# A one-column memset on GpSimd between any two of 6256 gathers in a four-round graph kernel

## What is computed

```python
h = relu(layernorm(x))
n1 = segment_sum(h[src], dst) / max(deg, 1)
n2 = segment_sum(n1[src], dst) / max(deg, 1)
x = x + 0.5 * n1 + 0.5 * n2
h = relu(layernorm(x))
for W_msg, W_edge, W_root, b in ((W1...), (W2...)):
    m = h[src] @ W_msg + edge_attr @ W_edge
    h = leaky_relu(where_finite(segment_max(m, dst)) + h @ W_root + b)
out = x + h
```

## Time and profile before

| | |
|---|---|
| median of 3 runs | 9557.13 us (9551.07 to 9563.12) |
| the profiled execution, its time | 9629.93 us |
| its span | 9628.2 us |
| granted TensorE clock, mean | 0.648 of full speed |
| busy share: TensorE matmul, VectorE, ScalarE, GpSimd | 58%, 34%, 16%, 67% |
| first to last gather of the four rounds | 61.0 to 2314.5, 2412.9 to 4651.5, 4777.2 to 7085.3, 7213.5 to 9521.9 us |

### The profile page before, as it was taken

One profiled execution on the slowest core, in us unless ns is written; L12 is line 12 of the kernel. 1 busy time (PEld: TensorE's weight loads), 2 busy tenths in 40 slices (PEclk: granted clock), 3 DMA queues, 4 the chain that ended last, 5 costly groups with the idle time before them and its releaser, 6 DMA issues.

```text
span 9628.2 us, 100471 instructions
## 1 busy us (share of the span) xinstructions
PE 5576.1 (58%) x25651; PEld 4095.6 (43%) x25651; DVE 3262.5 (34%) x6693; ACT 1500.7 (16%) x5073; POOL 6458.6 (67%) x6525
## 2 busy tenths in 40 slices
PE   2333333334233333333578877878887887887888
PEld 1222222223222222222555555555564555555556
DVE  4333333334333232323423333333332333333334
ACT  1000000001000000000322222222232222222223
POOL 5666666664666666666566666766656666666665
PEclk6555555556555555555767777777786777677776
DMA  3111111111111111111133333333323333333332
GB/s 79 35 34 34 34 34 34 34 35 39 47 35 34 34 34 35 34 34 35 46 76 77 77 77 77 78 80 78 77 64 71 80 78 77 77 77 77 77 81 64
DMA packets 309643, 548.56 MB, mean 57 GB/s; under 512 B 183464, under 2 KB 183464, under 8 KB 284712
## 3 DMA queue, kind: packets, MB, share of 16 engines
q0 software_dynamic: 200192, 307.90, 16.3%
q1 hardware_dynamic: 108804, 239.50, 9.7%
q10 hardware_dynamic: 548, 0.17, 0.0%
HBM read 522.27 MB, written 24.87 MB: 57 GB/s over the span
## 4 chain that ended last, share of the span: by engine, by line
another core or an unknown queue 29%; PE 26%; issue 9%; DVE 8%; DVEq 2%; ACT 1%; ACTq 1%; POOL 0%; DMA 0%; POOLq 0%; SPq 0%
PE ps L578 7%; PE ps L576 6%; PE ps L600 6%; PE ps L589 3%; DVE arena L799 3%; DVE comp L784 3%; PE ps L557 2%; DVE arena L767 2%; DVEq L257 1%; DVEq L784 1%; PE ps L662 1%; PE ps L638 0%; ACTq L257 0%; PE ps L675 0%
## 5 line engine op out<-in xcount | busy, mean ns | idle before, releaser
L374 POOL DMA_INDIRECT rows<-table,src_sb x6256 | 6273.4, 1003 | 2930.3 <-issue 1767.5
L557 PE MATMUL ps<-arena,rows 128*98 128x128 f32 (+1 forms) x6256 | 1418.1, 399 | 2967.0 <-DVE comp L784 2634.6
L557 PEld LDWEIGHTS ps<-arena,rows 128*98 128x98 f32 (+1 forms) x6256 | 1179.5, 254 | 3226.7 <-DVE comp L784 2836.3
L799 DVE TENSOR_TENSOR_SCAN arena<-arena,ps 96x512 f32<-96x512 f32 x782 | 996.6, 1274 | 3238.6 <-remote 1989.8
L784 DVE TENSOR_TENSOR comp<-comp,ps 98x128 f32 (+1 forms) x3128 | 893.6, 286 | 2878.4 <-remote 2317.0
L578 PEld LDWEIGHTS ps<-ident,rows 128*96 128x96 f32 x6256 | 950.4, 208 | 912.9 <-issue 912.7
L600 PE MATMUL ps<-arena 128*96 128x128 f32 x6256 | 1180.2, 352 | 108.6 <-issue 72.4
L578 PE MATMUL ps<-ident,rows 128*96 128x128 f32 x6256 | 1173.3, 344 | 54.2 <-issue 53.4
L576 PE MATMUL ps<-arena,we 32*96 32x512 f32 x1564 | 1143.7, 819 | 27.3 <-DMA rows<-table,src_sb 27.3
L600 PEld LDWEIGHTS ps<-arena 128*96 128x96 f32 x6256 | 1052.2, 228 | 129.6 <-issue 124.4
L767 DVE TENSOR_TENSOR arena<-iota_b,meta 128x512 f32<-128x512 bf16 x1564 | 1053.0, 673 | 59.6 <-issue 55.1
(11 more groups left out here) (84 smaller groups left out, 1026.0 us busy)
## 6 DMA issues: line engine op xcount, KB each, us to landing
arena<-flags SPq DMA_DIRECT2D x194, 768.0 KB
rows<-table,src_sb POOLq DMA_INDIRECT x6256
arena<-in_eat SPq DMA_DIRECT2D x194, 256.0 KB
table<-arena SPq DMA_DIRECT2D x56, 336.0 KB, 2.7
out<-xs SPq DMA_DIRECT2D x13, 336.0 KB
xs<-in_x SPq DMA_DIRECT2D x6, 672.0 KB, 5.9
arena<-flags SPq DMA_DIRECT2D x2, 576.0 KB
src_sb<-in_srcs SPq DMA_DIRECT2D x1, 782.0 KB, 5.2
```

Of the source, the lines that this page charges most:

```text
L374: pool.indirect_dma_start(rows[:, g % RING, j, 0:D], None, tables[r][:, :], bass.IndirectOffsetOnAxis(src_sb[:, c:c + 1], 0)).then_inc(lan ...
L557: m = pe.matmul(ps[0:w, at + k * P:at + (k + 1) * P], rows[:, j, k, 0:w], hot[:, j % HOTS, k, :], start=True, stop=True)
L799: dve.tensor_tensor_scan(run[:, slot % SCANS], fe[0:D, slot // UNIT, q * W:(q + 1) * W], ps[0:D, ROWS + slot % 2 * BANK:ROWS + slot % 2 * ...
```

## The change

A spare buffer of one float in each of 128 partitions is made. Behind every gather GpSimd clears it with a memset, which raises a semaphore of its own. From the second memset on, each one first waits until the memset before it has finished (of the same round, or for a round's first one, the last memset of the round before). Nothing reads the buffer.

```diff
+        spare = sb("spare", [P, 1])
...
+        spaced = sems("gathers_spaced", rounds)
...
                         pool.indirect_dma_start(rows[:, g % RING, j, 0:D], None, tables[r][:, :],
                                                 bass.IndirectOffsetOnAxis(src_sb[:, c:c + 1], 0)
                                                 ).then_inc(landed[r][g % RING], 16)
+                        if c or r:
+                            pool.wait_ge(spaced[r if c else r - 1], c if c else COLS)
+                        pool.memset(spare[:], 0.0).then_inc(spaced[r], 1)
```

## The result

The changed kernel takes 9576.69 us (median of 10 runs, 9560.97 to 9586.47) where the kernel before takes 9551.31 us on the same chip (10 runs, 9538.70 to 9563.12): a ratio of 1.0027 [1.0018, 1.0035], 25 us slower. The profiled execution took 9568.75 us. Every ratio here is between runs on one chip.

A forecast was written before the change was run, and what follows sets the result against it. An unnamed limit of 1.43 to 1.48 us per gather was taken as the bound, with 626 us of memsets absorbed by GpSimd's pauses; 9557 us plus 13 (+40 and -27) gave 9570 us, range 9230 to 10190.

The forecast's parts named there:

- The bound: In the four rounds, something unnamed serves 1.43 to 1.48 us per gather; GpSimd's pauses make up the rest.
- slack: GpSimd's pauses per gather beyond its own pace: 0.155, 0.146, 0.148 and 0.148 us in the four rounds.
- the memset's own cost: Behind each gather on GpSimd: 0.10 us per memset, bounds 0.03 and 0.40, 626 us in all.
- The absorption: The 626 us of memsets are taken from GpSimd's pauses, leaving 1.43 to 1.48 us per gather; chance 0.36.
- The two corrections: Memset time showing in the rounds, 0 to +81, taken +40 us; shorter VectorE tail at round ends, 0 to -40, taken -27.
- The wait: On GpSimd, each memset's wait for the memset before costs nothing, covered by the 0.95 us gather in between.
- the third rival: In the rounds, the limit counts more than gathers, or memset signals are held: +626 us, 10183 us; chance 0.22.
- The held word: Rival: TensorE's late slot-read signal passes during memsets and pauses go: -308 us, 9249 us; chance 0.22.
- The memset dearer than the slack: Rival: behind gathers a memset costs over 0.15 us; at 0.20 us, +317 us, 9874 us; chance 0.20.
- nothing is absorbed: In the rounds, all memset time shows, pauses as long as before: +626 us, 10183 us; chance 0.22.
- the limit also counts the memset or its signal: In the rounds, the memset's signal itself loads whatever holds TensorE's signals: +626 us, 10183 us; within a chance of 0.22.

The follow-up runs named there:

- the repeat: The kernel before, run again unchanged as its own control: 9635.72 us against 9635.64 us, ratio 1.0000.
- more loads: Kernel before plus one small SyncE load per group in rounds 0 and 1, with its own completion signals: 8522.03 us, ratio 1.0003.
- split gathers: Kernel before with each gather split in two of 64 rows, 12,512 gathers: 15759.89 us in the one run made, where before took 8519.14 us.

## Why the prediction was right, and which step of it was not

**The bound was read rightly, with one correction.** That no engine is full and that GpSimd's pauses make up what its pace is short of a limit held in every run with held signals: 0.13 us more per gather showed by 53 of 813 us with 192 bytes, 0.04 us less showed not at all with half the rows, and above the limit, with 512 bytes, pauses and late signals went. What the rows of before could not show is that the limit belongs to some chips only. It costs some 1020 to 1120 us there (9551 and 9636 against 8527 and 8519 us). That made the prediction's assumption riskier than it knew: on a chip of the other kind the kernel has no slack, and 0.10 us more in GpSimd's step would have shown in full. The slack itself was mis-sized in rounds 2 and 3: 0.148 us by GpSimd's pace of 1.329, 0.18 by the 1.295 us that it showed where nothing is held.

**The step that failed is the memset's own cost.** I took 0.10 us per memset, 626 us in all, between 0.03 and 0.40. It is 0.00, under the lower bound: the start-to-start time of gathers stayed 1.25 us. The 0.30 us behind a gather were read as a time that belongs to the gather, on top of which the memset comes; it is a time in which GpSimd can run a small instruction. It doesn't hide any length: 0.27 us of memset cost 0.13, 0.54 us cost 0.40, so 0.14 us is hidden in both. I had said that this time was what no row of before shows, and so it was. The Trainium skill, "Perfetto Trace Analysis", section "GPSIMD Engine Instruction", says to time such instructions from start to start, not by the reported span. The trace agrees: the recorded length is 0.116 us in the mean, the spacing says zero. The 0.03 us that I had by this way from the earlier trace rows were still too many, because there memset follows memset.

**The absorption was right, but this change did not use it.** The pauses were to shrink to about 1 us behind 20 gathers; the one shown stayed at 3.24 us, and on one chip their sum is 1021.1 us with a one-byte memset and 1030.6 without. With 192 bytes they shrank as foretold, by 0.13 us a gather.

**The two corrections, +40 and -27 us.** The first was 13% or less of 626 us. It has no base left, as nothing was added. What showed instead is 19 to 35 us that come with a memset that adds nothing to the step: 0.003 to 0.006 us per gather. The second, a shorter tail behind the last gather of a round, didn't come either: between the rounds' last and next first starts there are 353.8 us after and 352.3 in the earlier trace rows. Where time was really added, with 192 bytes, both are seen: the rounds grew by 9% of it, the last folds of round 0 end 7.1 us after the last gather (15.6 in the earlier trace rows, 21.3 in the repeat on that chip), and the stretches between the rounds are 15 us shorter.

**The wait** was put at nothing. That is right for the time, since taken away with the signals it gave nothing back, but not for every memset: the memset's own signal, which should have been seen after 0.95 us, came late in 44 places, up to 3.4 us behind the end of the memset, and 59.3 us of idle time stand before the memsets. That is the second half of the third rival (the signal "held by it"), in a small measure.

**The rivals.** The held word did not get through: the folds are 12.3 us late with memsets in the stream. The memset dearer than the slack is refuted for one column, and is what a memset of 512 bytes does. That nothing is absorbed could not be told from the change, which added nothing to absorb; the memset of 192 bytes refutes it (53 of 813 us). That the limit also counts the memset or its signal is refuted as far as 0.10 us per gather goes. In a form twenty times smaller it may be what is left: +25, +19 and +35 us in three measurements where signals are held, and none with two memsets where they aren't. That is a difference between chips in a kernel that isn't quite the change (which was not run on a chip of the other kind), so that the loss needs the limit is argued, not shown.

**The forecast.** 9570 us was 7 us under the 9577 measured. It is right in its bound, a limit per gather that GpSimd's small additions don't move. That it lies so close is luck: the 626 us weren't there and were struck out by an absorption that wasn't needed, and the +13 us of the two corrections, neither of which took place here, stand near the +25 us of a small loss that nothing in the rows pointed to.

**Open.** What the limit is, and why it is there on some chips only. It goes neither by rows nor by bytes. Gathers as such, the fixed set of completion signals of each, or the groups of four that all kernels here keep, are not told apart; the two kernels made for that, more loads and split gathers, ran where the limit is absent. Why it holds TensorE's signals back until GpSimd is quiet is open with it, and so is the source of the small loss per gather.

## What to carry to other kernels

Before an instruction on a queue is priced by its length, look at the gap that stands behind its neighbour: here a memset of 0.12 us behind a gather cost nothing, because it ran in a 0.30 us gap that was there anyway, and only what exceeded the gap had to be paid. An engine that pauses regularly on signals of consumers that aren't busy may be held by something slower than itself, as here; adding a known length to it (here 192 and then 512 bytes of memset) brackets the limit's pace, and a shortened step that brings nothing tells what the limit doesn't count. And where a limit has no name in the trace, run the unchanged kernel on more than one chip before arguing from it.

## What the runs showed of the hardware

- The same kernel takes 8519 and 8527 us on two chips and 9551, 9553 and 9636 us in three other measurements. The first have no pauses of GpSimd; the others are held to 1.43 to 1.48 us per gather.
- A gather of 128 rows takes 1.25 us from start to start and one of 64 rows 1.21 us; half the bytes per row change the kernel by 0.3%. So most of the price is that of the instruction, not of what it moves.
- Behind a gather GpSimd can run up to about 0.12 to 0.15 us of other work at no cost: one memset and 0.19 us, or two and 0.16 us, both give 1.25 us.
- Where TensorE's signals are late, GpSimd's own can be too: 44 of 6255 memsets began up to 2.3 us late at the semaphore of the memset before.
- Eight semaphore increments more per group on VectorE cost 41 us (0.6%) in a kernel in which VectorE waits most of the time.
